# DLRM tower: ten embedding fields looked up by one-hot matmul in place of eight, and a new order of the steps behind

## The reference

```python
e = jnp.stack([tbl_0[ids[:, 0]], ..., tbl_25[ids[:, 25]]], axis=1)
T = jnp.concatenate([dense[:, None, :], embs], axis=1)
Z = jnp.einsum('bnd,bmd->bnm', T, T)
z = Z[:, iu0, iu1]                       # n < m
h = jnp.concatenate([z, r_dense], axis=1)
h = jnp.maximum(h @ W_top1 + b_top1, 0.0)
h = jnp.maximum(h @ W_top2 + b_top2, 0.0)
y = h @ W_top3
```

## Time and profile before

| what | value |
|---|---|
| median of 3 runs | 124.29 us |
| the profiled execution's own time | 124.55 us |
| its span, first to last instruction | 122.6 us |
| TensorE busy (matmul) | 93.3 us, 76% |
| VectorE busy | 75.5 us, 62% |
| ScalarE busy | 73.7 us, 60% |
| GpSimd busy | 75.4 us, 62% (72 gathers: 73.3 us, and 21.6 us of gaps of 0.3 us between them) |
| matmuls of the one-hot lookup | 68 pairs, 57.5 us busy, pipelined |
| data moved | 13.64 MB, mean 111 GB/s |

### The profile page before, as it was taken

How to read it: one execution, slowest core, us unless ns; L and a number is a source line. 1 busy time by engine, 2 the same in 40 slices (tenths; PEclk the granted TensorE clock), 3 DMA queues, 4 the chain that set the end, 5 groups by cost and what they waited for, 6 DMA issues and landing times. The chain is left out here.

```text
span 122.6 us, 3575 instructions
## 1 busy us (share of the span) xinstructions
PE 93.3 (76%) x1460; PEld 76.8 (63%) x1460; DVE 75.5 (62%) x164; ACT 73.7 (60%) x154; POOL 75.4 (62%) x82
## 2 busy tenths in 40 slices
PE   5659988979789879956519798787947666579791
PEld 5547755646557658756408697676937456569680
DVE  4979999999999995036350993119920104880422
ACT  4097799998799978378380997209942105860000
POOL 4888777887887887787878787777878600040000
PEclk9999999999999999998555999999999999999999
DMA  1896786969899831121222122121222100000000
GB/s 50 244 311 214 259 262 203 289 184 275 184 241 345 267 85 43 43 70 47 66 61 70 50 67 62 51 64 48 64 62 65 48 21 5 8 19 1 0 5 0
DMA packets 7452, 13.64 MB, mean 111 GB/s; under 512 B 2378, under 2 KB 4108, under 8 KB 7308
## 3 DMA queue, kind: packets, MB, share of 16 engines
q1 hardware_dynamic: 5068, 8.67, 22.6%
q0 software_dynamic: 2368, 4.74, 14.3%
HBM read 13.16 MB, written 0.00 MB: 107 GB/s over the span
## 5 line engine op out<-in xcount | busy, mean ns | idle before, releaser
L301 POOL DMA_INDIRECT rows<-tbl,idx x72 | 73.3, 1018 | 22.9 <-issue 21.6
L353 PE MATMUL l<-hot,t_hi 128*128 128x512 f32 x68 | 29.4, 433 | 6.2 <-DVE hot L537 3.8
L537 DVE TENSOR_TENSOR hot<-ids_bc,rownum 128x512 fp32r<-128x512 int32 x51 | 32.3, 693 | 0.4 <-PE l L355 0.4
L355 PE MATMUL l<-hot,t_lo 128*128 128x512 f32 x68 | 28.1, 414 | 0.0
L419 DVE COPY Zlow<-gr 14x224 f32<-14x224 f32 x16 | 8.6, 540 | 22.2 <-PE gr L370 22.0
L353 PEld LDWEIGHTS l<-hot,t_hi 128*128 128x128 f32 x68 | 13.7, 201 | 13.5 <-issue 7.9
L370 PE MATMUL gr<-XT 128*32 128x26 f32 x1024 | 14.8, 202 | 8.4 <-issue 4.9
L370 PEld LDWEIGHTS gr<-XT 128*32 128x32 f32 x1024 | 12.7, 117 | 11.2 <-issue 7.0
L502 ACT COPY XT<-tp 128x512 f32<-128x512 f32 (+1 forms) x20 | 12.2, 654 | 10.6 <-PE tp L341 10.5
L341 PE MATMUL tp<-ident,rows 128*128 128x128 f32 x72 | 11.4, 295 | 7.4 <-DMA rows<-tbl,idx 3.7
L419 ACT COPY Zlow<-gr 14x224 f32<-14x224 f32 x16 | 8.7, 545 | 13.1 <-PE gr L370 12.9
(11 more groups left out here) (32 smaller groups left out, 62.5 us busy)
## 6 DMA issues: line engine op xcount, KB each, us to landing
ids_bc<-ids_oh SPq DMA_DIRECT2D x8, 256.0 KB, 4.1
table<-small SPq DMA_DIRECT2D x4, 512.0 KB, 4.1
table<-small SPq DMA_DIRECT2D x2, 640.0 KB, 5.6
rows<-tbl,idx POOLq DMA_INDIRECT x72, 3.2
w_sb<-w SPq DMA_DIRECT2D x1, 1024.0 KB, 8.6
table<-small SPq DMA_DIRECT2D x2, 320.0 KB, 5.4
w_sb<-w SPq DMA_DIRECT2D x1, 512.0 KB, 8.2
table<-small SPq DMA_DIRECT2D x2, 192.0 KB, 4.9
```

The costliest lines, as they stand in the source:

```text
L301: nc.gpsimd.indirect_dma_start(rows[:, t, place - FIRST, :], None, tbls[f], bass.IndirectOffsetOnAxis(ap=idx[:, t, f:f + 1], axis=0)).then ...
L353: nc.tensor.matmul(lookup_bank(i), t_hi[:, i % PARTS, c * D:(c + 1) * D], hot[:, k % HOTS, :], start=c == 0, stop=False)
L355: last = nc.tensor.matmul(lookup_bank(i), t_lo[:, i % PARTS, c * D:(c + 1) * D], hot[:, k % HOTS, :], start=False, stop=c == n - 1)
L537: nc.vector.tensor_tensor(hot[:, k % HOTS, :], ids_bc[:, i % IDS, :], rownum[:, v, c:c + 1].broadcast_to((OH_ROWS, BATCH)), ALU.is_equal). ...
```

## The change: what it does

- Two more fields, 11 and 13 (1,250 rows each), are looked up by one-hot matmul: 10 fields, 88 chunks. 16 fields are gathered: 64 gathers and four groups of four for each tile.
- VectorE's compare is a `tensor_scalar` (the ids as its one tensor input, the row number as a scalar of each partition) in place of a `tensor_tensor`.
- ScalarE makes every sixth hot in place of every fourth.
- `rows` steps inside the one-hot stage: all four groups of tile 0 and the first three of tile 1 (before: the five groups of tile 0).
- A new order behind it: both layers of tile 2 stand ahead of `rows(3, 3)` and of tile 3's grams.
- The last tile's products with the dense vector write to two older gram banks and the two `tp` banks, so they wait for tile 2's copies only; `layer1(3, 1)` follows without another tile's `layer2` between. The last tile's `h1` blocks alternate between VectorE and ScalarE, and its `h2` is one block on each.

```diff
-ONEHOT = [4, 5, 6, 12, 16, 23, 2, 9]
+ONEHOT = [4, 5, 6, 12, 16, 23, 2, 9, 11, 13]
-ACT_EVERY = 4
-ROWS_AFTER = {K_OH - 3: [0, 1], K_OH - 2: [2, 3, 4]}
+ACT_EVERY = 6
+ROWS_AFTER = {5: [(0, 0), (0, 1)], 6: [(0, 2), (0, 3)], 7: [(1, 0)], 8: [(1, 1), (1, 2)]}
...
-        steps += [("rows", 0, g) for g in ROWS_AFTER.get(i, [])]
-    steps += [("rows", 1, 0), ("rows", 1, 1), ("gram", 0, 0), ("gram", 0, 1), ("rows", 1, 2), ("gram", 0, 2),
-              ("rows", 1, 3), ("rows", 1, 4), ("gram", 0, 3)]
-    steps += [("gram", 1, 0), ("rows", 2, 0), ("gram", 1, 1), ("rows", 2, 1), ("gram", 1, 2), ("layer1", 0, 0),
-              ("layer1", 0, 1), ("rows", 2, 2), ("gram", 1, 3), ("rows", 2, 3), ("rows", 2, 4), ("layer2", 0, 0)]
-    steps += [("gram", 2, 0), ("gram", 2, 1), ("rows", 3, 0), ("gram", 2, 2), ("gram", 2, 3), ("layer1", 1, 0),
-              ("layer1", 1, 1), ("rows", 3, 1), ("rows", 3, 2), ("layer2", 1, 0), ("rows", 3, 3), ("layer1", 2, 0),
-              ("rows", 3, 4)]
-    steps += [("gram", 3, h) for h in range(2 * HALVES)]
-    steps += [("layer1", 2, 1), ("layer1", 3, 0), ("layer2", 2, 0), ("layer1", 3, 1), ("layer2", 3, 0)]
-    merged = {0: 0, 2: 1}
-    return [(kind, t, merged[i] if kind == "gram" else i) for kind, t, i in steps if kind != "gram" or i in merged]
+        steps += [("rows", t, g) for t, g in ROWS_AFTER.get(i, [])]
+    steps += [("gram", 0, 0), ("rows", 1, 3), ("gram", 0, 1), ("gram", 1, 0), ("rows", 2, 0), ("layer1", 0, 0),
+              ("gram", 1, 1), ("rows", 2, 1), ("layer1", 0, 1), ("layer2", 0, 0), ("rows", 2, 2), ("layer1", 1, 0),
+              ("layer1", 1, 1), ("rows", 2, 3), ("gram", 2, 0), ("layer2", 1, 0), ("gram", 2, 1), ("rows", 3, 0),
+              ("rows", 3, 1), ("layer1", 2, 0), ("rows", 3, 2), ("layer1", 2, 1), ("layer2", 2, 0), ("rows", 3, 3)]
+    steps += [("gram", 3, 0), ("gram", 3, 1), ("layer1", 3, 0), ("layer1", 3, 1), ("layer2", 3, 0)]
+    return steps
...
+            if u < GRAM_BANKS - HALVES:
+                return gr[:, u, :, :].rearrange("p q n -> p (q n)")[:, 0:P]
+            return tp[:, u - (GRAM_BANKS - HALVES), 0:P]
...
                 elif kind == "layer1" and t == TILES - 1 and i == 0:
-                    pe.wait_ge(gram_dve, HALVES * TILES)
-                    pe.wait_ge(gram_act, HALVES * TILES)
+                    pe.wait_ge(gram_dve, HALVES * t)
+                    pe.wait_ge(gram_act, HALVES * t)
+                    pe.wait_ge(tp_empty, banks)
...
                 elif kind == "layer1" and t == TILES - 1:
+                    pe.wait_ge(gram_dve, HALVES * TILES)
+                    pe.wait_ge(gram_act, HALVES * TILES)
...
+                elif kind == "layer1" and t == TILES - 1 and i == 1:
+                    act.wait_ge(l2_full, t)
+                    for u in range(1, BLOCKS, 2):
+                        act.wait_ge(l1_full, t + 1 + u)
+                        nc.scalar.activation(h1[:, u, :], l1_block(t, u), ACT.Relu).then_inc(h1_act, 1)
+                elif kind == "layer2" and t == TILES - 1:
+                    act.wait_ge(w2_in, 2 * 16)
+                    act.wait_ge(l3_full, t)
+                    act.wait_ge(l2_full, t + 1)
+                    nc.scalar.activation(h2[:, 1, :], l2_block(t, 1), ACT.Relu,
+                                         bias=tail_sb[:, 0, 1:2]).then_inc(h2_act, 1)
...
-                            nc.vector.tensor_tensor(hot[:, k % HOTS, :], ids_bc[:, i % IDS, :],
-                                                    rownum[:, v, c:c + 1].broadcast_to((OH_ROWS, BATCH)),
+                            nc.vector.tensor_scalar(hot[:, k % HOTS, :], ids_bc[:, i % IDS, :],
+                                                    rownum[:, v, c:c + 1], None,
                                                     ALU.is_equal).then_inc(hot_dve, 1)
```

More of the change, by code:

```diff
@@ L140, in split_parts, with by_both @@
     return i + min(i, HEADED) + (1 if i >= HEADED or c < HEAD else 2)
+def by_both(t, u):
+    return t == TILES - 1 and u % 2 == 1
 def units_ready(t, u):
-    return t + 1 + (u if t == TILES - 1 else 0)
+    if by_both(t, u):
+        return u // 2 + 1
+    return t + 1 + (u // 2 if t == TILES - 1 else 0)
 def by_scalar(k):
@@ L216, in dlrm_tower @@
         l1_full, h1_ready, l2_full = sem("l1_full"), sem("h1_ready"), sem("l2_full")
+        h1_act, h2_act = sem("h1_act"), sem("h2_act")
         h2_ready, l3_full, y_ready = sem("h2_ready"), sem("l3_full"), sem("y_ready")
@@ L227, in l1_block, with l2_block @@
                 return l1[:, u, :]
-            return gr[:].rearrange("p k q n -> p (k q n)")[:, u * BANK:u * BANK + P]
+            if u < GRAM_BANKS - HALVES:
+                return gr[:, u, :, :].rearrange("p q n -> p (q n)")[:, 0:P]
+            return tp[:, u - (GRAM_BANKS - HALVES), 0:P]
+        def l2_block(t, v):
+            if t == TILES - 1 and v:
+                return gr[:, GRAM_BANKS - HALVES, :, :].rearrange("p q n -> p (q n)")[:, 0:P]
+            return l2[:, v * P:(v + 1) * P]
         block = ctx.enter_context(nc.Block())
@@ L404, in _ @@
                         for u in range(BLOCKS):
-                            pe.wait_ge(h1_ready, units_ready(t, u))
-                            last = nc.tensor.matmul(l2[:, v * P:(v + 1) * P], w2_sb[:, u, v * P:(v + 1) * P],
+                            if by_both(t, u):
+                                pe.wait_ge(h1_act, units_ready(t, u))
+                            else:
+                                pe.wait_ge(h1_ready, units_ready(t, u))
+                            last = nc.tensor.matmul(l2_block(t, v), w2_sb[:, u, v * P:(v + 1) * P],
                                                     h1[:, u, :], start=u == 0, stop=u == BLOCKS - 1)
                     last.then_inc(l2_full, 1)
-                    pe.wait_ge(h2_ready, PIECES * (t + 1))
+                    pe.wait_ge(h2_ready, PIECES * t + (1 if t == TILES - 1 else PIECES))
+                    if t == TILES - 1:
+                        pe.wait_ge(h2_act, 1)
                     for v in range(PIECES):
@@ L555, in _ @@
                     else:
-                        for u in range(BLOCKS):
-                            dve.wait_ge(l1_full, units_ready(t, u))
+                        for u in range(0, BLOCKS, 2):
+                            dve.wait_ge(l1_full, t + 1 + u)
                             nc.vector.tensor_scalar(h1[:, u, :], l1_block(t, u), 0.0, None,
@@ L565, in _ @@
                     dve.wait_ge(l2_full, t + 1)
-                    for v in range(PIECES):
-                        nc.vector.tensor_scalar(h2[:, v, :], l2[:, v * P:(v + 1) * P], tail_sb[:, 0, v:v + 1], 0.0,
+                    for v in range(PIECES if t < TILES - 1 else 1):
+                        nc.vector.tensor_scalar(h2[:, v, :], l2_block(t, v), tail_sb[:, 0, v:v + 1], 0.0,
                                                 ALU.add, ALU.max).then_inc(h2_ready, 1)
```

## The result

The changed kernel takes 139.26 us (median of 4 runs, 137.06 to 140.0) against 124.47 us (4 runs). The ratio is 1.109, 95% interval 1.093 to 1.126; it leaves out disturbed runs, so it is a little under the quotient of the medians. Slower, as forecast, but by 14.8 us where the prediction had 6.6, and outside its range of 124 to 137. The profiled execution took 138.94 us, 7.7 us more than the 131.2 that the prediction's sum gave for a profiled one.

A forecast was written before the change was run, and what follows sets the result against it. Now bound by GpSimd's gathers until 100.47 us, then tile 3's tail; afterwards by TensorE's order: 55.4 to A, 56.3 to gram(3, 0), 16.0 tail, sum 127.7; with span and time offsets 131.2 profiled, 130.9 us predicted, range 124 to 137.

The forecast's parts named there:

- the named places: Behind the one-hot stage: TensorE idle 4 to 6 us ahead of layer1(0, 0) and of layer1(2, 0).
- The compare: VectorE in the one-hot stage: 0.40 us each, middle of 0.16 and 0.63, under the 0.45 it can bear.
- A: End of the one-hot stage, the last lookup copy: from 51.1 to 55.4 us, at least 54.4, upper end 58.4.
- tile 0's moves: Behind the one-hot stage: they land 14.5 us after A, and TensorE waits for them before layer1(0, 0).
- tile 2's wait: Ahead of layer1(2, 0): TensorE waits about 5.8 us for tile 2's moves, the dearest wait of the new order.
- tile 3's tail without layer2(2): From gram(3, 0) to the end: 16.0 us in place of 19.6, mostly because layer2(2) moves to the middle.
- the upper bound: A at 58.4, gram(0, 1) held, layer1(0, 0) and layer1(2, 0) up to 2.25 us slower each: some 139, cut to 134.5.
- The first rival: One-hot stage: compares slow the gathers, rows(1, 2) come 5.9 us late at 1.9 us a gather; 136.8 us; chance 0.13.
- The prediction's threshold: One-hot stage: above 1.64 us a gather, fifth to 28th, the rows for rows(1, 2) come too late for TensorE.
- The second rival: One-hot stage: the compare stays at 0.63 us, A comes at 68.4, 13.0 later; 143.9 us; chance 0.08.
- The third: A to gram(3, 0): under 49.7 us in place of 56.3, gathers stay the bound; time below 124.3; chance 0.12.
- No change: Whole kernel: within 1%, path at its lower bound and 1 to 2 us less at the waits; chance 0.09.

The follow-up runs named there:

- the filled waits: Idle transposes on TensorE at three places: added to the changed kernel 139.13 us, added to the control 135.44 us.
- the control: The changed kernel with one step moved, rows(1, 2) behind the last lookup in place of ahead of it: 138.66 us, ratio 1.120.
- the spaced order: The changed kernel's parts with a new step order, such as gram(1, 1) ahead of tile 0's layer1 and layer2(1) ahead of gram(2, 0): 123.06 us, ratio 0.992.
- both with late rows: The changed kernel with rows(1, 2) behind the last lookup, without idle transposes (138.66 us) and with them (135.44 us).

## Why the prediction was wrong

**What held.** The direction and its mechanism: the gathers leave the path, TensorE's walk through the new order sets the time, and its waits stand at the named places, with a shorter one than named only ahead of layer1(0, 0). The compare at 0.41 us (0.40 taken), A at 56.4 (55.4), tile 0's moves at the time computed (layer1(0, 0) 13.95 us behind A, 14.5 taken), tile 2's wait as the dearest (its layers' place is worth 9 to 10 us by experiment), tile 3's tail without layer2(2). That 0.40 came so near is partly luck: it was the middle between two bounds, 0.16 and 0.63, that lay far apart. The Trainium skill (VectorE: DVE Perf Modes, The perf-mode tier table) had the compare's price as an estimate of 0.33 to 0.42 us, and the trace agrees at its upper end, with 0.41 from start to start; one compare by itself is 0.48 to 0.49 us long.

**What failed: the size, by a term set to nothing.** The sum took every layer step at its full-clock price, and named the low clock only in the upper bound, for two halves, "not all at once". They came all at once. layer1(0, 0) +1.4, layer1 of tile 2 +2.5, and the last pairs with what follows +2.2, which no bound had: 6.1 of the 7.9 us that the sum fell short. (Of the last 2.2 the pairs themselves are 1.8: 4.5 us from their start to the second layer's, against 2.8 before.) The windows show these stretches at 0.50 to 0.60 of full clock right behind waits of 1.6 to 4.6 us. For two of the three the filled waits show it by experiment: layer1 of tile 2 went from 6.9 us in the control to 5.2 and the 24 pair matmuls from 4.2 to 2.7. For layer1(0, 0) it is read from the clock, and from the spaced order: there gram(1, 1) ran ahead of it in place of a wait, and its six pair matmuls took 0.85 us in place of 1.46. The one fill tried at it, in that order, held up the path. The rest, +1.0 at A, +1.2 and +0.6 between, is unsettled small change: grams of 2.2 and 2.4 us to their first copy where 1.92 stood (the first of them, at 74.06, at the low clock too), 1.4 us for a rows group and its copy where 1.15 stood.

The walk had the material for this. It found two open waits for moves, one of 5.8 us, and had the earlier trace rows beside them, a quiet stretch with the clock at 0.54. Each wait should have carried a price twice: its length, and the slower work behind it.

**The first rival** (gathers slowed by compares) is shown as a mechanism: the 64th gather 4.8 us late with the new compare, 0.5 with the old one, and the compare alone makes the kernel before 2% slower. That the longer stage or fuller queues delayed them is out: with the old compare the stage was longer still. The prediction's threshold was 1.64 us a gather; the mean from the fifth (8.23) to the 28th (43.86) was 1.55, against 1.39 before, so in the profiled execution it stayed just off the path. In the execution with the filled waits, with the same one-hot stage and a mean of 1.78, it was on it with 2.7 us. The Trainium skill (SBUF — State Buffer, Who interferes with whom) says that a two-port VectorE instruction that starts first blocks GpSimd's descriptor writing for its whole length. These runs agree that gathers lengthen (in the changed kernel from 0.94 to between 1.06 and 2.87 us), by 0.1 to 0.5 us each for the most part, which is up to the length of one compare (0.49). The longest, 1.9 us over, ran beside a row of ten compares; what held it so long is not shown.

**The second rival** was refuted for the change and priced by the old compare: A at 66.0, 9.6 us later where 13 was computed, and +7 us of time by the medians, +9 by the ratios (1.183 against 1.109). **The third,** faster, had no ground in this order; with another order the ten fields come to 0.992. **No change** was 1% to either side of before, and no execution of the changed kernel came below 137.06 us.

## What to carry to other kernels

When a bound is relaxed, walk the written order of the engine that takes over, step by step; the waits can be found that way before anything is built. Price the work right behind each open wait at the low clock as well, as a second case, until the trace shows which it is (in three places here it was the low one), and put other ready work, not a step that depends on the newest data, behind a slow handover. A faster instruction on an engine that was not the bound can still cost, through what it shares with the one that was.

## What the runs showed of the hardware that was not expected

- Work that computes nothing can pay: with 84 idle transposes the time was 135.44 us in place of 138.66, and the traces put 2.3 us of that to them. Where the wait is closed and the clock low, they hold up the path (20 in 4.3 us in one execution; what that costs in time is open).
- TensorE stops for up to 2.6 us, with no releaser in the profile, in or right behind grams of 128 short matmuls. A layer half between the last two grams removed such a stop of 2.35 us. The version with it is 2.4 us faster by the medians (120.48 against 122.88 us) and 1.8 by the ratios to its own runs of before (0.975 and 0.990, whose intervals touch); in the traces the last third-layer matmuls start 15.6 us behind gram(3, 0) in place of 17.7. The stops keep their place: gram(0, 1) is split behind its 71st matmul in the changed kernel, in the one with the old compare and in both with late rows, whatever the times around it, and gram(2, 1) behind its 38th in all four kernels with eight fields. That speaks for the supply of instructions and against a wait for data, but it is argued, not shown.
